# Graph attention, second layer: x parts of a head every second unit, q of heads 2 and 3 in two buffers, s as half lines, the mean on ScalarE, a prologue that reads x from the residual

## The reference

```python
h = maximum(layernorm(x), 0)
q = (h @ W).reshape(B, N, 4, 64)
e = e_src[:, :, None, :] + e_dst[:, None, :, :]   # q . a_src, q . a_dst
e = where(e >= 0, e, 0.2 * e)
attn = softmax(where(adj > 0, e, -9e15), axis=2)
x = x + elu(attn @ q)
```

## Time and profile before

| | |
|---|---|
| median of 3 executions | 5143.4 us (5140.66 to 5144.62) |
| profiled execution | 5128.5 us |
| its span, first to last instruction | 5126.7 us |
| mean granted TensorE clock | 0.975 |
| second layer, from its first DMA | 3436.9 us to the end |
| first pick of batch 0 | 3520.85 us |

### The profile page before, as it was taken

The page is one execution under the profiler, slowest core; times in us unless marked ns, Lnnn a source line. Parts: engine busy times, 40 slices in busy tenths (PEclk is TensorE's granted clock), DMA queues, the critical chain, the costliest instruction groups (busy, mean ns, idle before and its releaser), DMA issues. The chain is left out here.

```text
span 5126.7 us, 139194 instructions
## 1 busy us (share of the span) xinstructions
PE 4799.6 (94%) x56352; PEld 4402.8 (86%) x56352; DVE 3755.8 (73%) x7147; ACT 2899.6 (57%) x3121; POOL 1412.9 (28%) x1661
## 2 busy tenths in 40 slices
PE   6999999999999999999999999956988988989899
PEld 4998899889898899889988989855988988989899
DVE  6666667666676667666766666647888888898898
ACT  4444444444444444444444444426877877888787
POOL 3343344334343344334433433330000000000000
PEclk9999999999999999999999999978999999999999
DMA  5000100010001010010001000022111121121210
GB/s 205 17 18 17 30 26 18 22 26 26 22 18 26 18 30 18 17 30 26 18 22 26 26 18 13 22 82 68 42 60 63 38 69 55 44 75 37 66 63 28
DMA packets 110193, 198.02 MB, mean 39 GB/s; under 512 B 7088, under 2 KB 93488, under 8 KB 103088
## 3 DMA queue, kind: packets, MB, share of 16 engines
q1 hardware_dynamic: 98464, 144.80, 8.4%
q0 software_dynamic: 11024, 43.53, 3.3%
HBM read 112.53 MB, written 38.03 MB: 29 GB/s over the span
## 5 line engine op out<-in xcount | busy, mean ns | idle before, releaser
L577 PEld LDWEIGHTS outs<-v_s,probs 128*128 128x128 f32 x16384 | 1977.1, 192 | 111.6 <-issue 27.6
L690 ACT ACTIVATE slot<-slot,shift 128x1024 f32<-128x1024 f32 x1024 | 1111.6, 1088 | 1586.7 <-PE slot L567 1586.7
L577 PE MATMUL outs<-v_s,probs 128*128 128x128 f32 x16384 | 1991.5, 275 | 5.0 <-DVE ctx_part L847 5.0
L831 DVE SCALAR_TENSOR_TENSOR probs<-slot,bound 128x1024 f32<-128x1024 f32 x1024 | 1250.7, 1224 | 708.1 <-ACT slot L690 707.6
L1391 ACT ACTIVATE cond<-s_all,d_sign 128x1024 bf16<-128x1024 f32 x1024 | 1123.9, 1142 | 218.5 <-DVE u L1546 213.0
L566 PE MATMUL slot<-q_hl,k_hl 128*128 128x512 f32 x2048 | 894.4, 437 | 41.5 <-DVE probs L831 27.0
L393 POOL TENSOR_TENSOR ctx_sum<-ctx_sum,ctx_part 128x256 f32<-128x256 f32 x896 | 650.1, 731 | 1017.5 <-DVE ctx_part L847 1017.1
L1292 PE MATMUL sums<-x_mixed,u 128*128 128x130 f16 x8192 | 811.9, 223 | 18.6 <-issue 18.6
L1546 DVE TENSOR_TENSOR u<-cond,mask 128x1024 f16<-128x1024 bf16 x1024 | 690.9, 681 | 179.6 <-PE sums L1296 105.2
L567 PE MATMUL slot<-q_hl,k_hl 128*128 128x512 f32 x2048 | 804.1, 393 | 0.0
L1296 PE MATMUL sums<-x_mixed,mask 128*128 128x65 f16 x8192 | 782.0, 196 | 0.0
(11 more groups left out here) (137 smaller groups left out, 3663.4 us busy)
## 6 DMA issues: line engine op xcount, KB each, us to landing
q_hl<-q_hl POOLq DMA_DIRECT2D x128, 256.0 KB, 3.7
s_all<-s_turned SPq DMA_DIRECT2D x32, 1024.0 KB, 5.1
xs<-in_x SPq DMA_DIRECT2D x32, 512.0 KB, 4.4
x<-y SPq DMA_DIRECT2D x32, 512.0 KB, 3.1
x_s<-x SPq DMA_DIRECT2D x32, 512.0 KB, 5.8
o_s<-x SPq DMA_DIRECT2D x16, 1024.0 KB, 6.3
out<-o_s SPq DMA_DIRECT2D x16, 1024.0 KB, 4.7
probs<-in_adj SPq DMA_DIRECT2D x11, 1024.0 KB, 5.1
```

Of the source, the lines that this page charges most:

```text
L577: end = nc.tensor.matmul(outs[i % OUTS][:, q, :], probs[:, i % PROBS, r, q * P:(q + 1) * P], v_s[:, c * JC + r, h * E1:h * E1 + P], start= ...
L690: nc.scalar.activation(slot[:, :, :], slot[:, :, :], ACT.Exp, bias=shift[:, 0:1], scale=SCALE).then_inc(act_done, 1)
L831: nc.vector.scalar_tensor_tensor(probs[:, i % PROBS, :, :], spot(kind, "step", s, i)[:, :, :], P_LOW, bound[:, (i // H) % 2, :, :], ALU.ma ...
```

## The change

- `weigh` stands in unit 6 (head 0 of the next batch) and in units 0, 2 and 4 (heads 1 to 3), `low` and `back` in units 7, 1, 3 and 5. The prologue builds head 0 alone.
- q of heads 0 and 1 is in `q_near`, q of heads 2 and 3 in `q_far`, two buffers by the batch's parity; so VectorE's and ScalarE's loops have three turns of two batches.
- s comes as half lines of 0.5 MB, one a unit.
- POOL computes the negative mean, ScalarE adds it (`center`, in steps 4, 5, 6 and 9), `normalize` is gone, and the inverse deviation is the scale of `keep_q`, whose instruction for q becomes two.
- In the prologue x is read from the residual o_s; the four strip loads of batch 0 are gone, and the mask comes in two halves once the residual is there.

```diff
+CENTER_AT = (4, 5, 6, 9)
...
-        rstd = sb("rstd1", [P, IT])
+        rstd = sb("rstd1", [P, 2, IT])
+        mean_neg = sb("mean_neg", [P, IT])
-        q_s = sb("q_s", [P, NT, H * E1])
+        q_near = sb("q_near", [P, NT, 2 * E1])
+        q_far = sb("q_far", [P, 2, NT, 2 * E1])
...
-        s_all = sb("s_all", [P, 2, N])
+        s_all = sb("s_all", [P, HALVES, HALF])
...
-            def load_s(b, h, guard):
-                for half in range(2):
-                    sp.wait_ge(s_stored[half], (b + 1) * (NS // 2) * IT * 16)
+            def load_s(b, m, guard):
+                if m == 0:
+                    for half in range(2):
+                        sp.wait_ge(s_stored[half], (b + 1) * (NS // 2) * IT * 16)
                 if guard:
-                    sp.wait_ge(cond_ready, (b * H + h - 1) * HALVES * NT)
-                sp.dma_start(s_all[:, h % 2, :], row_on_all(s_dram[b][h])).then_inc(s_loaded[h % 2], 16)
+                    sp.wait_ge(cond_ready, (b * UNITS + m - 1) * NT)
+                first = m % HALVES * HALF
+                sp.dma_start(s_all[:, m % HALVES, :], row_on_all(s_dram[b][m // HALVES][first:first + HALF]))\
+                    .then_inc(s_loaded[m % HALVES], 16)
...
-            for k in range(NS):
-                load_strip(0, k, k >= 2)
-                if k >= 2:
-                    store_s(0, k - 2)
-            store_s(0, NS - 2)
-            store_s(0, NS - 1)
-            spread_d(0)
-            load_s(0, 0, False)
-
             for half in range(HALVES):
                 load_res(0, half, False)
+            for k in range(NS):
+                store_s(0, k)
+            spread_d(0)
+            for m in range(HALVES):
+                load_s(0, m, False)
             def batch(b, first, last):
                 for m in range(UNITS):
-                    if m in (0, 2, 4):
-                        load_s(b, m // HALVES + 1, not (first and m == 0))
+                    if m < UNITS - 1 and not (first and m == 0):
+                        load_s(b, m + 1, True)
                     if m < NS and not last:
-                        load_strip(b + 1, m, True)
+                        load_strip(b + 1, m)
                     if m < HALVES and not first:
                         store_out(b - 1, m)
                         load_res(b, m, True)
...
-                    if m == 6 and not last:
+                    if m == UNITS - 1 and not last:
                         load_s(b + 1, 0, True)
...
-            pool.dma_start(mask16[:, :, :], mask_dram).then_inc(mask_loaded, 16)
-            nc.gpsimd.memset(lift[:, :], LIFT)
...
+            pool.wait_ge(res_loaded[1], 16)
+            nc.gpsimd.memset(lift[:, :], LIFT)
+            for half in range(HALVES):
+                cols = slice(half * HALF, (half + 1) * HALF)
+                pool.dma_start(mask16[:, :, cols], mask_dram[:, :, cols]).then_inc(mask_loaded[half], 16)
             def inverse_std(pb, k):
                 pool.wait_ge(moments_done, pb * NS + k + 1)
-                nc.gpsimd.tensor_tensor(rstd[:, :], moments[:, :, 1], eps1[:, :], ALU.add).then_inc(var_eps_done, 1)
+                if not (isinstance(pb, int) and pb == 0 and k == 0):
+                    pool.wait_ge(centered, 2 * (pb * NS + k))
+                nc.gpsimd.tensor_tensor(mean_neg[:, :], moments[:, :, 0], neg_one[:, :], ALU.mult).then_inc(mean_neg_done, 1)
+                if not (isinstance(pb, int) and pb == 0 and k < 2):
+                    pool.wait_ge(pro_free, pro_freed(q_use(pb, k, IT - 1) - 2 * STRIP_PRO))
+                nc.gpsimd.tensor_tensor(rstd[:, k % 2, :], moments[:, :, 1], eps1[:, :], ALU.add).then_inc(var_eps_done, 1)
                 pool.wait_ge(var_eps_done, pb * NS + k + 1)
-                nc.gpsimd.tensor_tensor(rstd[:, :], rstd[:, :], neg_half1[:, :], ALU.pow).then_inc(rstd_done, 1)
+                nc.gpsimd.tensor_tensor(rstd[:, k % 2, :], rstd[:, k % 2, :], neg_half1[:, :], ALU.pow).then_inc(rstd_done, 1)
...
             def transposes(pb, k, pair):
-                if pair == 0:
-                    pe.wait_ge(norm_done, pb * NS + k + 1)
+                pe.wait_ge(centered, 2 * (pb * NS + k) + pair + 1)
...
+            def center(pb, k, t):
+                if t == 0:
+                    act.wait_ge(mean_neg_done, pb * NS + k + 1)
+                src = xs[:, k % 2, t, :]
+                if isinstance(pb, int) and pb == 0:
+                    src = o_s[:, k * IT + t, :]
+                    if k >= 2 and t == 0:
+                        act.wait_ge(pro_filled, t_use(0, k - 2, T_PAIRS - 1) + 1)
+                op = nc.scalar.activation(xs[:, k % 2, t, :], src, ACT.Identity, bias=mean_neg[:, t:t + 1])
+                if t % 2:
+                    op.then_inc(centered, 1)
+
-            def keep_q(pb, k, t):
+            def keep_q(pb, odd, k, t):
                 if k == 0 and t == 0 and not (isinstance(pb, int) and pb == 0):
-                    act.wait_ge(x_mul_done, pb * H)
+                    act.wait_ge(x_mul_done, (pb - 1) * H + 2)
+                if t == 0:
+                    act.wait_ge(rstd_done, pb * NS + k + 1)
                 act.wait_ge(pro_filled, q_use(pb, k, t) + 1)
                 tile = k * IT + t
                 acc = bank(k, T_PAIRS + t)
-                nc.scalar.activation(q_s[:, tile, :].rearrange("p (h e) -> p h e", e=E1)[:, :, 0:D],
-                                     acc[:, 0:F].rearrange("p (h d) -> p h d", d=D), ACT.Copy)
-                nc.scalar.activation(sd[:, tile, :, :].rearrange("p s h -> p (s h)"), acc[:, F:WIDE], ACT.Copy).then_inc(pro_free, 1)
+                for side, q_side in enumerate((q_near[:, tile, :], q_far[:, odd, tile, :])):
+                    nc.scalar.activation(q_side.rearrange("p (h e) -> p h e", e=E1)[:, :, 0:D],
+                                         acc[:, side * 2 * D:(side + 1) * 2 * D].rearrange("p (h d) -> p h d", d=D),
+                                         ACT.Identity, bias=zero[:, 0:1], scale=rstd[:, k % 2, t:t + 1])
+                nc.scalar.activation(sd[:, tile, :, :].rearrange("p s h -> p (s h)"), acc[:, F:WIDE], ACT.Identity,
+                                     bias=zero[:, 0:1], scale=rstd[:, k % 2, t:t + 1]).then_inc(pro_free, 1)
...
+            for t in range(IT):
+                center(0, 0, t)
             for k in range(NS):
                 for pair in range(T_PAIRS):
                     relu_t(0, k, pair)
+                if k < NS - 1:
+                    for t in range(IT):
+                        center(0, k + 1, t)
                 for t in range(IT):
-                    keep_q(0, k, t)
+                    keep_q(0, 0, k, t)
                 keep_s(0, k)
...
-            high(0, 1, False)
...
+                        if begins and j in CENTER_AT:
+                            center(b + 1, k, CENTER_AT.index(j))
...
                         if ends and j in (7, 8, 10, 12):
-                            keep_q(b + 1, k - 1, (7, 8, 10, 12).index(j))
-                        if j == 15 and m >= 6 and not last:
-                            high(b + 1, m - 6, True)
-                        if j == 15 and m < 2:
-                            high(b, m + 2, not first)
+                            keep_q(b + 1, 1 - odd, k - 1, (7, 8, 10, 12).index(j))
+                        if j == 15 and m == 6 and not last:
+                            high(b + 1, 0, True)
+                        if j == 15 and m in (0, 2, 4):
+                            high(b, m // 2 + 1, not first)
...
-            batch(0, True, False)
-            with act.Fori(1, B - 1) as b:
-                batch(b, False, False)
-            batch(B - 1, False, True)
+            batch(0, 0, True, False)
+            with act.Fori(0, (B - 2) // 2) as n:
+                for odd in (1, 0):
...
-            nc.vector.memset(q_s[:, :, :], 1.0).then_inc(ones_ready, 2)
+            nc.vector.memset(q_near[:, :, :], 1.0)
+            nc.vector.memset(q_far[:, :, :, :], 1.0).then_inc(ones_ready, 2)
...
             def statistics(pb, k):
-                dve.wait_ge(x_loaded[k % 2], (pb * (NS // 2) + k // 2 + 1) * 16)
+                if isinstance(pb, int) and pb == 0:
+                    dve.wait_ge(res_loaded[k // 2], 16)
+                    src = o_s[:, k * IT:(k + 1) * IT, :]
+                else:
+                    dve.wait_ge(x_loaded[k % 2], ((pb - 1) * (NS // 2) + k // 2 + 1) * 16)
+                    src = xs[:, k % 2, :, :]
+                if not (isinstance(pb, int) and pb == 0 and k == 0):
+                    dve.wait_ge(moments_done, pb * NS + k)
                 for t in range(IT):
-                    last = nc.vector.bn_stats(stats[:, t, :], xs[:, k % 2, t, :])
+                    last = nc.vector.bn_stats(stats[:, t, :], src[:, t, :])
...
             def aggregate(pb, k):
                 dve.wait_ge(stats_done, pb * NS + k + 1)
+                if not (isinstance(pb, int) and pb == 0 and k == 0):
```

(45 more changed lines are left out.)

35 lines of the change are left out of this document (18 added, 17 removed).

## The result

The changed kernel takes 5058.48 us (median of 4 executions, 5054.78 to 5075.05) against 5142.03 (5140.45 to 5144.62) for the kernel before, executed beside it: a ratio of 0.9846, 95% interval 0.983 to 0.9863. The profiled execution took 5075.05 us with a span of 5073.2, that of before 5128.5 with 5126.7. So the two profiles differ by 53.5 us, the medians by 83.6: the profiled execution of the changed kernel was the slowest of its four, 16.6 us over their median, and that of before lay 13.5 under its median.

A forecast was written before the change was run, and what follows sets the result against it. TensorE bounds units 2 to 4, VectorE units 1, 6 and 7, issue waits unit 0. Batches -31.5, last batch +2, prologue -16.8: about -46 us, 5097 against the median 5143.4; 8 in 10 from 5055 to 5130.

The forecast's parts named there:

- The prologue: Ahead of the first pick: earlier start, slower strips and one head less together give -16.8 us, first pick near 3504.
- Start: Prologue: first transposes at 3450 to 3454 instead of 3467.83, -15 us, bounds -18 and -8.
- Strips: Prologue: four strips take 31.8 us instead of 26.3 with ScalarE's added work, +5.5 us, bounds 0 and 8.
- That rival: Prologue doesn't gain: mask issues hold POOL 10 us or the late mask gates the first pick; 5109 us, chance 0.07.
- Unit 7: Each batch's unit 7 loses its products and their stop, 24.8 us becoming 21.8, -3.0, with VectorE's 21.0 as floor.
- Unit 1: Each batch's unit 1 loses normalization and products on VectorE: 23.5 us against 27.5, -4.0.
- ScalarE heads the queue: Rival: in units 2 to 4 ScalarE, waiting for mean_neg at centering, is the slower side; 5181 us, chance 0.07.
- ScalarE's load: ScalarE's work per unit: 26.4 us in units 2 and 4, 24.4 in unit 3; 0.8 us a batch charged.
- Units 2 and 4: Products at steps 9 and 10 bring a shortened TensorE stop: +1.1 us each, bounds 0 and 3.8.
- the rival on the clock: The clock falls in units 2 and 4 behind the new stops: 27 us, time 5124 us, chance 0.16.
- Unit 0: Issue waits set each batch's unit 0 and stay; -0.5 us for the clock window carried over from unit 7's stop.
- The rival that half the transfer would shorten it: Unit 0 shrinks with the line of s half as large, five more batches by 6 us: 5067 us, chance 0.12.

The follow-up runs named there:

- e5: The changed kernel with mean_neg computed by VectorE at step 2 instead of by POOL: 5045.43 us, ratio 0.9823 to the kernel before.
- e6: The changed kernel with the centerings in steps 6 to 9 instead of 4, 5, 6 and 9: 5048.39 us, ratio 0.9827 to the kernel before.
- e11: The changed kernel with mean_neg on VectorE and the batches of TensorE, ScalarE and VectorE written out without loops: 4988.3 us, ratio 0.9735 to the kernel before.
- e3: The changed kernel with normalization (mean and deviation) back on VectorE: 5059.89 us, ratio 0.9842 to the kernel before.
- the square: Old or new x-part schedule, normalize on VectorE or mean on ScalarE; pick to end: e9 1611.3, e3 1570.5, e4 1589.7, e1 1567.7, changed kernel 1572.4 us.
- e1: The changed kernel run again, unedited: 5067.0 us, ratio 0.9853 to the kernel before.
- e9: The changed kernel with the old schedule of the x parts and normalization on VectorE both put back: 5111.08 us, ratio 0.9965 to the kernel before.
- e4: The changed kernel with the x parts built on the old schedule, in units 6, 7, 0 and 1: 5101.7 us, ratio 0.9926 to the kernel before.
- e7: The changed kernel with TensorE's loop in three turns of two batches instead of seven of one: 5016.17 us, ratio 0.976 to the kernel before.
- e8: The changed kernel with TensorE's batches written out without a loop and mean_neg on VectorE: 4996.1 us, ratio 0.9724 to the kernel before.
- e2: The kernel before with the new prologue alone, mask in one transfer and two heads built ahead: 5117.63 us, ratio 0.9949 to the kernel before.
- e10: The changed kernel with VectorE's differences and copy of the x parts at steps 5 to 7 instead of 2 to 4: 5058.39 us, ratio 0.9875.

## Why the prediction was right, and where it was not

The sign, the parts and their order held. The sum of the traces was forecast at -46 us and is -53.5. The median was forecast at 5097 (5055 to 5130) and came out at 5058.48, near the low end. That is under the 5075 to 5118 which the prediction worked out from its bounds; only the wider range of 8 in 10 holds it.

The batch's -4.8 for a forecast -4.5 is in part luck: unit 1 gained 1.2 us less than forecast, and against that stand 1.3 less lost in units 2 and 4 and 0.5 more gained in unit 7. Batch 0, where unit 1's product was short, gained 8.0. Two of the prediction's own signs failed: ScalarE does stand idle at the centering above 2 us (5.1), and in one batch, by the same wait, TensorE is idle in unit 3 (25.1 of 27.3 us busy).

*The prologue*, forecast -16.8, measured -20.0. Start: -15 forecast, -17.5 measured, inside its bounds. Strips: +5.5 forecast, +5.8 measured (32.1 us). Second head: -7.3 forecast, -8.3 measured. The mask issues took 2.43 us for both (forecast 0.655 to 2.2 each) and the mask gated nothing. That rival is out.

*Unit 7*, forecast -3.0, measured -3.5. "It can't be shorter than VectorE's 18.3 + 2.7 = 21.0" was wrong: 20.5. VectorE is ahead of TensorE at the unit's start and carries work over the boundary: its busy time in the stretch is 17.91 in batch 2 and 20.32 in batch 1, not 21.0 in each. A sum of work per unit is a floor only for a unit that has to start and end together.

*Unit 1*, forecast 23.5, measured 25.2. The estimate of VectorE's work was right: where POOL's product is short the unit takes 22.3 and 22.9, and 23.1 or less in e5, e6 and e11. What it lacked is a wait of ScalarE at centering.

*That wait* is the mechanism of the rival "ScalarE heads the queue": centering waits for mean_neg. The rival put it in units 2 to 4, by ScalarE's load, with POOL's operation at 0.56 us. It came in unit 1, the lightest of them for ScalarE, by POOL's operation at 4.58. It reached 5.1 us and cost 25.7 - 22.9, about 3 us a batch in five of seven batches. The step that failed is the price of POOL's operation, taken from one row beside VectorE. That row stands beside the same succession, pick, difference, pick, and was one of its short cases; the long one, 4.67 us, was in the trace of before, once in 28. The Trainium skill, "SBUF — State Buffer", section "Who interferes with whom", has a GpSimd operation blocked for the whole VectorE instruction that holds the port; here the trace goes beyond it: it was held through six such instructions in a row, and in other cases of the same succession it was not.

*Units 2 and 4*, forecast +1.1 each for a stop, measured +0.3 and +0.6, with TensorE busy 24.73 of 24.89 and 25.11 of 25.47 in batch 2 and the clock at 1.00 in both units of all seven batches. Half a us of unit 4's is again a held product: 25.5 us in the two batches where it took 2.28, 24.9 or 25.2 in the others. So no stop and no low window: the rival on the clock is out. The estimate took the 2.08 us of unit 1 as the nearest case, but there VectorE was out of lead by three kinds of side work, as the prediction had seen; in these units it seems not to have been, which no run tests. The last batch, forecast +2, came to +2.8.

*ScalarE's load*, forecast 24.4 us in unit 3 and 26.4 in units 2 and 4, measured 24.56, 24.00 and 23.57, with TensorE at its side full and some of the work carried into unit 5 (24.34). Moving the mean there was costed about right: 0.446 us for a part of q (forecast 0.435), 0.348 for s and d (0.33), 0.498 for a centering (0.46). Yet it gained nothing that shows once the schedule had been moved (e3). The prediction added normalization's 1.4 us and the products' 2.3 in unit 1; by the square the two gains don't add up. The Trainium skill, "ScalarE: Activation LUTs", section "Rules for kernel authors", sends such adds to VectorE; e3 and e1 say that on this schedule both places are equal in the batches, e9 and e4 that on the old one ScalarE is better by 22 us.

*Unit 0*, forecast as now (-0.5), measured 0.0. The rival that half the transfer would shorten it is out: the lines of s are half as large and the unit is the same. The waits follow the jump (e7, e8, e11). The Trainium skill, "Runtime: NRT & Kernel Launch", section "Instruction fetch mechanics", puts such a wait on the taken branch; these runs agree, with unit 0 falling from 33 us to 22.

*The size of the median's gain*, 83.6 us for 53.5 in the traces. The prediction saw that before's profiled execution was 14.9 under its median and set the change against the median, but its terms came from that favourable execution all the same. e2, with the batches of before, has 1615.6 us from the pick to the end, 163.2 at a lowered clock; the profile of before 1605.9 and 142.4. Against e2 the batches gain 43 to 48 us, which with 19 of the prologue makes 62 to 67. e1's ratio, 0.9837 to 0.987, is 67 to 84 us. What lies between, and why one execution differs from the next, is not settled.

## What to carry to other kernels

- Look for work that two engines do against each other at a unit's border before moving work from one to the other: spreading one engine's bursts over the units gave 41 us, moving work off that engine 22 alone and nothing measurable on top.
- A tiny operation of POOL that another engine waits for is a risk beside a run of VectorE's two-operand instructions, short in one batch and ten times as long in the next: look at its longest case and not at one row or the mean, and take it off POOL or let the other engine wait for it some steps later. And where an engine waits for "issue" right behind a loop's jump, write the batches out before tuning anything else in that unit: that was worth 57 to 61 us together with the move of mean_neg, more than all parts of the change in the batches.
- Take the terms of a sum from more than one execution where its profile lies off the median.

## What the runs showed of the hardware

- POOL's product of 128x4 f32 took 0.20 us in the prologue. Beside VectorE's instructions with both operands in SBUF it took 0.47 in 20 of 28 cases, 2.28 in two and 4.58 in six, and every long case ended as VectorE's first instruction with an operand in PSUM started. With the differences moved three steps it was 0.474 at most (e10).
- A jump back of TensorE's loop cost 6.13 and 2.66 us of issue in batch 2, and 10.2 us at a granted clock of 0.50 that begin within the first of these waits. Unit 0 is 33.2 us with the jumps of all three engines and 22.5 without any (e11). The same code written out eight times showed 2.0 us of issue waits on TensorE over the whole layer.
- A transfer of 64 KB landed in 3.2 us ahead of the 8.4 MB mask; issued behind it, it kept VectorE waiting 17.27 us.
